# Shared-expert units across the batch boundary, and the gate steps cut finer

## What is computed

```
x = x + xattn(layernorm(x), ctx, ctx, ...)      # 8 heads of 32
x = x + ffn(layernorm(x), ...)                  # 2 shared experts, 2 of 8 routed ones

# xattn: gates from [q, k, v]
ig = ifg @ igate_w.T + igate_b
log_f = log_sigmoid(ifg @ fgate_w.T + fgate_b)
cs = cumsum(log_f)
log_D[s, t] = cs[s] - cs[t] + ig[t]             # t <= s
D = exp(log_D - max_t log_D)
C = (q k^T / sqrt(32)) * D
h = C / (max(|sum C|, exp(-max log_D)) + eps) @ v

# shared expert: for each of 2 experts, H = 1024
h_s += gelu(rmsnorm(u) @ W1_s + b1_s) @ W2_s + b2_s
```

## Time and profile before

| | |
|---|---|
| runs shown | 1430.29, 1432.65, 1432.75 us; median 1432.65 |
| the profiled execution | 1436.01 us, span 1434.3 us |
| mean granted clock | 0.951 |
| busy: PE, DVE, ACT, POOL | 1170.9, 1026.1, 793.5, 389.5 us |
| one full pass (456.7 to 555.8 us): PE, DVE, ACT, POOL busy | 84.8, 68.8, 48.8, 21.3 of 99.1 us |

### The profile page before, as it was taken

How to read it: one execution, slowest core, us unless ns; L and a number is a source line. 1 busy time by engine, 2 the same in 40 slices (tenths; PEclk the granted TensorE clock), 3 DMA queues, 4 the chain that set the end, 5 groups by cost and what they waited for, 6 DMA issues and landing times. The chain is left out here.

```text
span 1434.3 us, 22326 instructions
## 1 busy us (share of the span) xinstructions
PE 1170.9 (82%) x7861; PEld 1008.2 (70%) x7861; DVE 1026.1 (72%) x2507; ACT 793.5 (55%) x1454; POOL 389.5 (27%) x397
## 2 busy tenths in 40 slices
PE   0363698797897987997978988599999999999996
PEld 0142477576676666775766777589888999899886
DVE  2356659568567676595684654588898889888984
ACT  2101355444553554554544443488888887888785
POOL 2312122041041121221410201144334433443343
PEclk9986799999999999999999998799999999999998
DMA  4899910000010010000000000677777777777772
GB/s 125 220 265 273 288 61 30 30 30 30 30 59 30 20 41 30 30 31 30 30 15 15 31 19 27 213 206 194 194 218 210 198 190 214 216 198 194 205 220 24
DMA packets 172563, 168.08 MB, mean 117 GB/s; under 512 B 48362, under 2 KB 159860, under 8 KB 172452
## 3 DMA queue, kind: packets, MB, share of 16 engines
q1 hardware_dynamic: 120884, 109.43, 25.3%
q10 hardware_dynamic: 37264, 38.54, 10.5%
q0 software_dynamic: 14304, 18.69, 6.3%
HBM read 109.42 MB, written 57.22 MB: 116 GB/s over the span
## 5 line engine op out<-in xcount | busy, mean ns | idle before, releaser
L1233 DVE TENSOR_TENSOR wlo<-raw,whi 128x512 fp32r<-128x512 f32 x312 | 228.2, 732 | 35.1 <-ACT whi L1184 31.4
L1155 PE MATMUL bank<-xhi,whi 128*128 128x256 f32 x624 | 178.8, 287 | 25.5 <-issue 20.2
L1206 ACT ACTIVATE hraw<-bank,b 128x256 f32<-128x256 f32 x312 | 148.2, 475 | 86.2 <-PE bank L1155 53.1
L1273 DVE TENSOR_TENSOR hlo<-hraw,hhi 128x256 fp32r<-128x256 f32 x312 | 183.1, 587 | 17.5 <-ACT hhi L1209 5.7
L973 PE MATMUL bank<-whs,shared_hhi 128*128 128x256 f32 x512 | 150.0, 293 | 50.1 <-DVE shared_hlo L727 50.1
L1135 PE MATMUL bank<-whi,hhi 128*128 128x256 f32 x624 | 180.3, 289 | 12.8 <-issue 11.4
L523 ACT ACTIVATE shared_hraw<-bank,b1s 128x512 f32<-128x512 f32 x128 | 88.1, 688 | 180.8 <-PE bank L988 171.4
L1155 PE MATMUL bank<-xlo,whi 128*128 128x256 f32 x624 | 175.3, 281 | 0.0
L1155 PE MATMUL bank<-xhi,wlo 128*128 128x256 f32 x624 | 175.1, 281 | 0.0
L1135 PE MATMUL bank<-whi,hlo 128*128 128x256 f32 x624 | 173.4, 278 | 0.0
L1135 PE MATMUL bank<-wlo,hhi 128*128 128x256 f32 x624 | 173.3, 278 | 0.0
(11 more groups left out here) (248 smaller groups left out, 2834.7 us busy)
## 6 DMA issues: line engine op xcount, KB each, us to landing
raw<-in_L_ffn_W_r_dram SPq DMA_DIRECT2D x78, 1024.0 KB, 7.8
sorted_tokens<-base ACTq DMA_DIRECT2D x1, 33540.0 KB, 137.6
xt<-sorted_tokens SPq DMA_DIRECT2D x39, 260.0 KB
big<-in_L_ffn_W_s_dram SPq DMA_DIRECT2D x4, 1024.0 KB
xb<-in_x_dram SPq DMA_DIRECT2D x8, 512.0 KB, 4.6
cb<-in_ctx_dram SPq DMA_DIRECT2D x8, 512.0 KB, 3.6
xr<-in_x_dram SPq DMA_DIRECT2D x8, 512.0 KB, 3.6
out_dram<-base ACTq DMA_DIRECT2D x8, 512.0 KB, 2.9
```

What stands on the lines that cost most here:

```text
L1155: last = nc.tensor.matmul(ub[:, 0:T], w[i][:, wsl], x_[i][:, k, :], start=k == 0 and t == 0, stop=k == KD - 1 and t == 2)
L1206: nc.scalar.activation(hraw[:, m % NHB, :], psum[m % NU][:, 0:T], ACT.Gelu, bias=b1[i][:, m:m + 1]).then_inc(t_gelu, 1)
L1233: nc.vector.tensor_tensor(wlo[i][:, psl], raw[i][:, psl], whi[i][:, psl].bitcast(fp32), ALU.subtract).then_inc(t_wlo, 1)
L1273: nc.vector.tensor_tensor(hlo[:, m % NHB, :], hraw[:, m % NHB, :], hhi[:, m % NHB, :].bitcast(fp32), ALU.subtract).then_inc(t_hlo, 1)
```

## The change

`ORDER` gets a new order, with nine front steps (all F) where there were six; two steps of DVE's front are cut (the second scan apart from the first; the casts and the exponent operand apart from the exponent arguments); units run on over the batch's end, so that `second` of units 14 and 15 stands behind the ups of units 0 and 1 of the next batch; and `finish(b - 1)` stands behind unit 1.

```diff
-        ORDER = "S 0 H 0 U A 1 U F 1 U Q 2 U F 2 B U P 3 U 3 D U G T E U T U T U R V U V U V U R U W U X C U".split()
+        ORDER = ("S 0 H 0 U A 1 U F 1 U Q 2 U F 2 B U P 3 U 3 D F U T E U T U F T U V U V U F V U F W U F X U F U F").split()
...
                     if units:
                         parts["unit"](b, k)
+                        if b > 0 and k == LAG - 1:
+                            parts["finish"](b - 1)
                         k += 1
...
-                elif step in "FGRC":
+                elif step == "F":
...
-            if units:
-                parts["finish"](b)
...
             side_by_side(parts, B - 1, back=False, front=False)
+            parts["finish"](B - 1)
...
                     own.end()
                     yield
                     yield
+                    yield
                     sc.wait_ge(earg_ready, b + 1)
                     nc.scalar.activation(eexp[:, :], earg[:, :], ACT.Exp).then_inc(eexp_ready, 1)
+                    yield
+                    yield
                     yield
...
                 def unit(b, k):
                     sc.wait_ge(up_done, U * b + k + 1)
-                    if k >= NHB:
+                    h = (U * b + k) % NHB
+                    if U * b + k >= NHB:
                         sc.wait_ge(unit_done, U * b + k - NHB + 1)
...
                     sc.wait_ge(xraw_ready, b + 1)
+                    if b > 0:
+                        sc.wait_ge(up_done, U * b)
                     nc.scalar.copy(xhs[:, :, :], unT[:, :, :]).then_inc(xhs_ready, 1)
...
                     own.done(stt(rows[FG:KE, :], att_bank[3][IG:IG + HR, :], ig_bias[:, :], cs[:, :],
                                  ALU.add, ALU.subtract))
+                    yield
                     own.done(nc.vector.tensor_tensor_scan(rows[0:HR, :], rows[FG:KE, :], rows[FG:KE, :],
                                                           -3.0e38, ALU.max, ALU.max))
...
                     ts(earg[:, 0:NW], earg[:, 0:NW], 0.0, None, ALU.min).then_inc(earg_ready, 1)
+                    yield
...
                     own.done(nc.vector.tensor_copy(low16[0:HR, :], rest[0:HR, 1, :]))
+                    yield
...
                 def second(b, k):
 
                     pe.wait_ge(hlo_ready, U * b + k + 1)
+                    if k == 0 and b > 0:
+                        pe.wait_ge(fin_ready, b)
...
-                    if k >= LAG:
-                        second(b, k - LAG)
-                    if k == U - 1:
+                    if U * b + k >= LAG:
+                        second(*divmod(U * b + k - LAG, U))
+                    if U * b + k == U * B - 1:
                         for late in range(U - LAG, U):
                             second(b, late)
```

More of the change, by code:

```diff
@@ L520, in unit @@
                     sc.wait_ge(up_done, U * b + k + 1)
-                    if k >= NHB:
+                    h = (U * b + k) % NHB
+                    if U * b + k >= NHB:
                         sc.wait_ge(unit_done, U * b + k - NHB + 1)
-                    nc.scalar.activation(hraw[:, k % NHB, :], up_bank[k % 2][:, :], ACT.Gelu,
+                    nc.scalar.activation(hraw[:, h, :], up_bank[k % 2][:, :], ACT.Gelu,
                                          bias=b1s[:, k // M, k % M:k % M + 1]).then_inc(gelu_done, 1)
                     sc.wait_ge(gelu_done, U * b + k + 1)
-                    nc.scalar.copy(hhi[:, k % NHB, :], hraw[:, k % NHB, :]).then_inc(hhi_ready, 1)
+                    nc.scalar.copy(hhi[:, h, :], hraw[:, h, :]).then_inc(hhi_ready, 1)
                 def finish(b):
@@ L725, in unit @@
                 def unit(b, k):
+                    h = (U * b + k) % NHB
                     dve.wait_ge(hhi_ready, U * b + k + 1)
-                    tt(hlo[:, k % NHB, :], hraw[:, k % NHB, :], hhi[:, k % NHB, :].bitcast(fp32), ALU.subtract
-                       ).then_inc(hlo_ready, 1)
+                    tt(hlo[:, h, :], hraw[:, h, :], hhi[:, h, :].bitcast(fp32), ALU.subtract).then_inc(hlo_ready, 1)
                 def finish(b):
@@ L968, in second @@
                     pe.wait_ge(hlo_ready, U * b + k + 1)
-                    e, m = k // M, k % M
+                    if k == 0 and b > 0:
+                        pe.wait_ge(fin_ready, b)
+                    e, m, n = k // M, k % M, (U * b + k) % NHB
                     wsl = slice(WN + m * D, WN + (m + 1) * D)
@@ L973, in second @@
                             last = mm(down_bank[j // 2][:, (j % 2) * D:(j % 2 + 1) * D],
-                                      h[:, k % NHB, j * P:(j + 1) * P], w[:, e, wsl],
+                                      h[:, n, j * P:(j + 1) * P], w[:, e, wsl],
                                       start=k == 0 and t == 0 and j % 2 == 0, stop=k == U - 1 and t == 2,
@@ L981, in unit @@
                         pe.wait_ge(xls_ready, b + 1)
-                    if k >= 2:
+                    if U * b + k >= 2:
                         pe.wait_ge(gelu_done, U * b + k - 1)
```

## The result

| | median | runs | ratio to before, 95% interval |
|---|---|---|---|
| before | 1432.65 us | 1430.29 to 1434.56 | |
| changed | 1446.52 us | 1440.55 to 1447.28 | 1.0085 [1.0058, 1.0111] |

The change makes the kernel slower by 0.6 to 1.1%. Its five runs lie in two groups, 1440.55 and 1441.12, and 1446.52 to 1447.28. The profiled execution is the fastest of them (span 1438.8 us), so against the profiled execution of before (1436.01) only 4.5 us are to be explained in the traces, not 13.9.

A forecast was written before the change was run, and what follows sets the result against it. A PE chain, a VectorE chain and a 6.9 us handover were taken to bound each period. Batch 0 +2.4, five periods +14.5, end +2.5 and start -1.6 gave +17.8 on 1432.65: 1450.5 us, range 1432 to 1463.

The forecast's parts named there:

- main term: At each period's end, the next exponents start at 661.7 against 658.82: +2.9 us a period.
- The flush taken out: At the batch's end, exponents could start when VectorE's chain ends, at 651.9 and not 658.82: 6.9 us a period saved.
- The two seconds: Ahead of the next batch's PV matmuls, 2.80 us of moved work fills PE's 2.25 us wait; 0.55 us delays.
- The wait for the logarithm: At the gates' step ahead of x1, VectorE waits 2.9 us for ACT and ends 2.4 us late.
- PE stands 7.1 us at un: Ahead of unit 13, PE waits 7.1 us for un; the clock halves and eight transposes take 1.97 us.
- VectorE waits 3.3 us for unit 13 and 2.9 for unit 14: Behind the transposes of un, VectorE stands some 3.3 us at unit 13, then about 2.9 at unit 14.
- The casts 4.56 us and the operand 2.81 to 661.7: At the period's end, casts of 4.56 us, unit 15's low part and the 2.81 us operand end at 661.7.
- under 99: Sign against the forecast: a period under 99 us, above all if PE doesn't stand at L968; 102 us was expected.
- the clock does not fall: Rival: PE's clock stays full or falls late at un; -0.1 us a period, about 1432 us; chance 0.09.
- Start -1.6, end +2.5, batch 0 +2.4: Outside five ordinary periods: run-up gains 1.6 us, the last two batches lose 2.5, batch 0's period loses 2.4.
- more than forecast: Rival: the clock also falls after the state matmuls, exponents and scores cost some 3 us a period: 1468 us; chance 0.05.
- faster: Rival: VectorE's chain keeps 43.2 us, the 6.9 us handover goes less 0.55, six periods: 1395 us; chance 0.16.

The follow-up runs named there:

- The continuation alone: Changed kernel with the front steps back in their old places in ORDER, units still running over the batch's end: 1415.42 us, ratio 0.9863.
- the fastest kernel: Changed kernel with front steps in their old places, units running over the batch's end, and the rows' transposes ahead of the logits: 1395.64 us, ratio 0.9728.
- the second series: The changed kernel run again, unchanged, for a second profile: 1466.48 us, ratio 1.0227 to the kernel before.
- the same 18 matmuls: Changed kernel with 18 extra 128x512 bf16 matmuls on PE ahead of its wait for un, in six full passes: 1453.55 us, ratio 1.0134.
- the other kernel: Kernel with the 18 extra matmuls ahead of un, and POOL's scatters moved behind the copies and masks of the next values: 1442.58 us, ratio 1.0055.

## Why the prediction came out

The direction and the range were right: 1450.5 us with 1432 to 1463, measured 1446.5. But the nearness is partly luck. The sum was made for the profiled execution, and there it was +17.8 where the traces show +4.5. Its main term, +2.9 us in every period, came only in the first and, for another reason, in the last. The measured +13.9 are those 4.5, the 6.0 by which the changed kernel's median lies above its profiled execution, and the 3.4 by which the median before lies below its own. No trace explains these 9.4.

*The flush taken out: 6.9 us a period.* Right as a size, as far as it can be told from two moves together. The continuation alone gave 4 us with half-clock state matmuls, and 6.6 (99.05 to 92.4) with the rows' transposes ahead of the logits as well.

*The two seconds, 0.55 us.* From the exponents to those of the third chunk 21.35 us became 21.6: 0.3. The add into base cost nothing in the full periods; in the last batch PE waits 0.83 us for it.

*The wait for the logarithm, 2.9 us and VectorE 2.4 late.* The wait is 3.22 us. ACT went from Abs at 616.58 to the logarithm at 620.52 in 3.94 us, which two loads of 1.28 and two steps of 0.68 and 0.63 fill. The drain of some 1.38 us that the Trainium skill, "ScalarE: Activation LUTs", What ACT_TABLE_LOAD costs, puts on each load is not in this trace. By itself the move of the wait costs 9.5 us, 1.6 a period. Part of the wait only moved: unit 9's cast, behind ACT's same loads, was done at 623.80, and VectorE took it at 625.19, so without the wait at x1 it would have gained 1.4 us and not 3.2.

*PE stands 7.1 us at un, the clock at half, transposes 1.97 us.* 6.83, 0.50 and 1.97. `un` was forecast for 81.1 us into the period and came at 81.3. This step is the main cost: +42.8 us when put in alone, with the first scan ahead of `un`.

*VectorE waits 3.3 us for unit 13 and 2.9 for unit 14.* 2.27 and 2.67. The first is smaller since the clock was back 2.7 us behind the wait's end: unit 13's up took 2.15 us, not the 2.80 of half clock throughout. In batch 0 it was not back, and the waits were 3.02 and 3.75.

*The casts 4.56 us and the operand 2.81 to 661.7: the term that was mis-sized.* They took 3.30 and 2.17. The 4.56 of the earlier trace rows was read beside POOL's weighting, and in the changed kernel the casts come when POOL is done (at 650.18, after 3.57 us of weighting and not 5.14). VectorE's timeline before, and after:

```profile
645.16 0.74 DVE L636 CAST big<-big 56x512 bf16<-56x512 f32 x1
...
647.72 0.75 DVE L639 CAST big<-big 24x512 bf16<-24x512 f32 x1
```

```profile
651.88 0.42 DVE L645 CAST big<-big 56x512 bf16<-56x512 f32 x1
...
653.54 0.41 DVE L648 CAST big<-big 24x512 bf16<-24x512 f32 x1
```

These 1.9 us and the earlier return of the clock make up the forecast's +2.9 a period against a measured 0.2 (+0.63 in four). The period "under 99" that would have refuted the mechanism did not come, but at 99.1 this sum came out where the rival "the clock does not fall" put it, with the clock falling all the same.

*Start -1.6, end +2.5, batch 0 +2.4.* -5.25, +3.25, +2.63. Of the start, 2.25 us lie ahead of the first exponents (81.28 for 83.53), and they are not the change's: the first gate matmuls, before and changed:

```profile
55.89 5.80 PE L889 MATMUL bank<-qcT,gate_w 128*56 128x512 f32 x8 [0.68 <-ACT qcT L481]
```

```profile
55.79 3.64 PE L899 MATMUL bank<-qcT,gate_w 128*56 128x512 f32 x8 [0.68 <-ACT qcT L482]
```

Over all fourteen traces they take 3.64 us in seven and 5.4 to 5.9 in the other seven, whatever the order. The other 3.0 (77.05 us to the next exponents, 80.05 before) are the rows ahead of the logits; the fastest kernel has them too, at 77.04, and the continuation alone, without them, is at 79.90. Batch 0 came near its +2.4 since there the clock stayed low, as the forecast had it for every period; the end's parts were not taken apart.

*The rival "more than forecast", 0.05.* It is real: exponents and scores at half clock behind a wait of 1.72 us, +2.8 us, in one of six periods of the first trace; behind the same wait the clock stayed at full in three other periods. I had held the gap for too short. Two more of these, two more periods like batch 0's, or a late start in two periods, would lift a run by 5 to 7 us, near the 6 of the median over the profiled execution; which it was is open.

*What no step had.* The transposes of q ahead of unit 6 were costed at nothing, with their gain in time only. They also take away the cover of ACT's late start, which was to be seen in the profile before: ACT's copy at 603.95, 2.54 us behind PE's end, with "remote" as what it waited for, and 0.46 us of PE's wait left. That is 20 us when put in alone, and much of what sets the second series 20 us above the first, at 1466.5 and above my range.

*The rival "faster", 0.16*, was the right story for the part of the change that carries units over the batch's end. I had priced the two halves of the diff only together.

## What to carry to other kernels

Cost a step's wait where it will stand, and its duration with the neighbours that it will have there: the same casts took 0.74 us beside POOL and 0.41 behind it. Before a step is moved ahead of a filler unit, look at what that unit has been hiding, late starts of another engine included, for that becomes a wait of PE and then of its clock. And when a change has two parts, run each by itself: here one is worth 1.4% (2.7% with one more step moved), and the other more than takes it back.

## What the runs showed that was not expected

- One program took 1446.5 us in one series and 1466.5 in another, with the kernel before within 3 us in both. The second series' trace has a start of ACT 1.9 to 2.8 us behind PE's signal in each full period (1.3 to 2.8 over all traces), at times of VectorE too, while POOL issues scatters; the first's has none. What in the scatters does it, and why one trace is free of it, stays open.
- The clock fell in waits of 6.83 and 2.93 us and in a row of five of 1.1 to 2.2 us; a wait of 2.94 behind the same 18 matmuls left it at full in three of six periods of one kernel (1.09 to 1.10 us for the transposes), and in the other kernel the transposes were at half in five of six (1.97 us). The length of one wait doesn't decide it.
- Casts to bf16 of 24 and 56 partitions by 512 took mostly 0.73 to 0.75 us while POOL's multiplications ran and 0.41 to 0.42 otherwise. The eight scalings of the operand took 2.81 us where they began beside POOL and 2.17 otherwise, and POOL's own six multiplications 5.14 us beside VectorE's casts and 3.57 without them.
- Within one trace, the half clock went on for 2.7 us behind a wait of 6.83 us in one period and for 5.6 us behind the same wait in another.
